# Holding two of ten gather chunks until a Gram product is done, in a DLRM tower kernel

## The reference

```
e = stack([tbl_f[ids[:, f]] for f in range(32)], axis=1)     # 2048 x 32 x 128
dot = einsum('bfd,bgd->bfg', e, e)                           # 2048 x 32 x 32
z = dot[:, iu, ju]                                           # upper triangle, 496 values
h = concatenate([z, dense_ctx], axis=1)                      # 512 values
h = maximum(h @ W_top1 + b_top1, 0)                          # 512
h = maximum(h @ W_top2 + b_top2, 0)                          # 256
y = h @ W_top3                                               # 1
```

## Time and profile before

| | us |
|---|---|
| median of 3 runs | 624.3 (624.0 to 625.61) |
| the profiled execution | 620.44 |
| its span, first to last instruction | 618.5 |
| PE busy | 458.5 (74%) |
| POOL busy | 324.9 (53%) |
| DVE busy | 259.9 (42%) |
| ACT busy | 126.9 (21%) |
| mean granted TensorE clock | 0.865 of full speed |

### The profile page before, as it was taken

How to read it: one execution, slowest core, us unless ns; L and a number is a source line. 1 busy time by engine, 2 the same in 40 slices (tenths; PEclk the granted TensorE clock), 3 DMA queues, 4 the chain that set the end, 5 groups by cost and what they waited for, 6 DMA issues and landing times.

```text
span 618.5 us, 11060 instructions
## 1 busy us (share of the span) xinstructions
PE 458.5 (74%) x4564; PEld 413.5 (67%) x4564; DVE 259.9 (42%) x489; ACT 126.9 (21%) x220; POOL 324.9 (53%) x324
## 2 busy tenths in 40 slices
PE   0785310697787795987967886877969878679998
PEld 0785300587676794867856785857858777669977
DVE  3685000277232641536523472425425364328340
ACT  2361100022211221112301221112212113113323
POOL 6887777156643664446646566436655466450000
PEclk9798655698978897978979978779989789799999
DMA  7996312023312252113422223122521234121000
GB/s 162 244 231 178 101 51 54 10 63 82 76 38 48 56 93 55 34 43 76 72 51 59 51 71 77 34 42 55 98 51 34 47 72 79 48 59 19 2 2 1
DMA packets 31292, 42.08 MB, mean 68 GB/s; under 512 B 11076, under 2 KB 24140, under 8 KB 31272
## 3 DMA queue, kind: packets, MB, share of 16 engines
q1 hardware_dynamic: 18936, 20.64, 16.2%
q0 software_dynamic: 10240, 20.99, 13.9%
q10 hardware_dynamic: 2096, 0.17, 0.3%
HBM read 41.77 MB, written 0.01 MB: 68 GB/s over the span
## 4 chain that ended last, share of the span: by engine, by line
PE 53%; issue 19%; another core or an unknown queue 12%; POOL 7%; DVE 5%; ACT 2%; DMA 2%; DVEq 0%; POOLq 0%
PE sel_ps L280 19%; PE gram_ps L299 17%; PE work_ps L333 7%; POOL gathered L240 7%; PE work_ps L262 4%; DVE onehot L602 3%; DVE pairs L613 2%; PE work_ps L324 1%; DMA gathered<-table,tile_ids 1%; ACT rows_T L458 1%; PE work_ps L407 1%; PE work_ps L316 1%; PE work_ps L341 1%; PE work_ps L416 1%
## 5 line engine op out<-in xcount | busy, mean ns | idle before, releaser
L240 POOL DMA_INDIRECT gathered<-table,tile_ids x320 | 324.7, 1015 | 229.3 <-issue 94.2
L280 PE MATMUL sel_ps<-onehot,table_hi 125*128 125x256 f32 x768 | 205.8, 304 | 47.0 <-DVE onehot L602 26.4
L602 DVE TENSOR_SCALAR onehot<-id_rows,row_no 128x512 fp32r<-128x512 int32 x384 | 160.5, 484 | 129.2 <-remote 85.1
L280 PE MATMUL sel_ps<-onehot,table_lo 125*128 125x256 f32 x768 | 201.0, 298 | 0.0
L280 PEld LDWEIGHTS sel_ps<-onehot,table_hi 125*128 125x128 f32 x768 | 159.3, 207 | 49.4 <-issue 27.7
L299 PE MATMUL gram_ps<-rows_T 128*64 128x64 f32 x1920 | 104.0, 259 | 95.0 <-issue 88.2
L299 PEld LDWEIGHTS gram_ps<-rows_T 128*64 128x64 f32 x1920 | 88.6, 168 | 112.0 <-issue 111.7
L280 PEld LDWEIGHTS sel_ps<-onehot,table_lo 125*128 125x128 f32 x768 | 159.3, 207 | 0.0
L613 DVE STREAM_TRANSPOSE pairs<-gram_ps 32x1024 f32<-32x1024 f32 x60 | 74.7, 1246 | 194.4 <-PE gram_ps L299 193.5
L458 ACT ACTIVATE rows_T<-work_ps 128x512 f32<-128x512 f32 x80 | 47.4, 593 | 187.6 <-PE work_ps L262 139.6
L467 ACT ACTIVATE rows_T<-sel_ps 128x512 f32<-128x512 f32 x48 | 30.6, 637 | 173.1 <-PE sel_ps L280 79.4
(11 more groups left out here) (26 smaller groups left out, 90.2 us busy)
## 6 DMA issues: line engine op xcount, KB each, us to landing
id_rows<-ids_selected SPq DMA_DIRECT2D x48, 256.0 KB
gathered<-table,tile_ids POOLq DMA_INDIRECT x320
pairs<-tables_selected SPq DMA_DIRECT2D x6, 448.0 KB
x<-tables_selected SPq DMA_DIRECT2D x6, 448.0 KB
w_sb<-w SPq DMA_DIRECT2D x1, 1024.0 KB
w_sb<-w SPq DMA_DIRECT2D x1, 512.0 KB
pairs<-tables_selected SPq DMA_DIRECT2D x6, 52.0 KB
x<-tables_selected SPq DMA_DIRECT2D x6, 52.0 KB
```

The source lines that it names most:

```text
L240: nc.gpsimd.indirect_dma_start(gathered[:, t, g, :], None, tables_gathered[g], bass.IndirectOffsetOnAxis(ap=slot_id, axis=0)).then_inc(chu ...
L280: last_op = nc.tensor.matmul(sel_ps[:, u % 2, e, :], part[0:SEL_P, 2 * u + e, k, :], onehot[0:SEL_P, h, kk, e, :], start=(e == 0 and k == ...
L602: last_op = nc.vector.tensor_scalar(onehot[:, h, kk, :, :].rearrange("p e s -> p (e s)"), id_rows[:, slot, :, :].rearrange("p e s -> p (e ...
```

## The change

GpSimd's stream gets two more waits for every pair after pair 0. Before the first gather of chunk 5 it also waits until the first gram of the pair before is done, and before the first gather of chunk 9 until its second gram is done. Nothing else is different; no instruction changes its place.

```
                         if p > 0:
 
                             pool.wait_ge(chunk_turned, 2 * NC * (p - 1) + NC * t + c + 1)
+                            if NC * t + c in (5, 9):
+
+                                pool.wait_ge(gram_done, 2 * (p - 1) + (1 if c == 0 else 2))
                         pool.nop(nofuse=True)
```

## The result

The changed kernel is slower: 638.8 us median (635.2 to 642.2, four runs) against 624.9 us for the kernel before, ratio 1.0244 (95% interval 1.0199 to 1.029). I had forecast 609 us, faster, with a range up to 643 us; the time is near that of my rival A (641 us).

What follows compares the result with a forecast made beforehand. The prediction took PE's stream, with holes in grams beside gathers, as the bound: 620.44 - 12.6 (six pairs) - 2.5 (pair 0) = 605.3 us, plus 3.9 to the median gives 609.2 us; range 577 to 643.

Steps and rivals of the forecast that it cites:

- rival A: Longer gather runs, over the second gram and after it, cost more than free first grams bring: 641 us; chance 0.27.
- First grams: First grams of pairs 1 to 6, freed of eight gathers: -8.0 us a pair, saving between 5.2 and 9.0.
- Second grams: Sixteen held gathers run into second grams of pairs 1 to 6: loss 3.9 us a pair, between 2.3 and 5.3.
- Second gram to next first gram: Stretch behind second grams, run of 12 gathers, not 8: loss 2.0 us a pair, from gain 3.8 to loss 5.2.
- Sum of a pair: Each loop pair: -8.0 + 3.9 + 2.0 = -2.1 us; six pairs give -12.6 us.
- Pair 0: First gram ends 20.0 us earlier, but moved gathers over its second gram give that back: -2.5 us (-4.5 to +1.3).
- B: PE is held only inside grams and late wake-ups shrink with the waits: -10.4 us a pair, 557 us; chance 0.15.
- C: Gathers do not stop a gram, only their time of day coincides, so nothing moves: 624 us; chance 0.05.
- The rule: DMA never contends with a compute engine, so gathers do not stop grams and holding them returns nothing: time as before.

Runs made afterwards that it cites:

- Hold5_7: Changed kernel with chunk 7, not 9, waiting for the second gram: 627.4 us, ratio 1.0062 to the kernel before on chip 10; 0.9988 on chip 1.
- hold5: Changed kernel with only the wait before chunk 5 kept: ratio 0.9987 to the kernel before, where that takes 467 us.
- hold9: Changed kernel with only the wait before chunk 9 kept: ratio 0.9987 to the kernel before, where that takes 467 us.
- paced: Kernel before with a small GpSimd write and wait behind each gather from pair 1 on: 578.9 us, 0.9568 on chip 14; 527.2 us, 1.1299 on chip 3.

## Why the prediction was wrong

The sum said -15.1 us, and +14.9 was measured: 30.0 us apart. Of these, the second grams make 17.9, the six stretches after them 18.6, and the last stretch and the tail 0.9; the first grams give back 5.9 and pair 0 1.5. So two terms failed, by about as much each.

*First grams: right.* -8.0 forecast, (23.9 - 77.8) / 6 = -9.0 measured. Each fell to the row without gathers, though the load of id rows stayed; that load cost these grams nothing.

*Second grams: the first step that failed.* I had both ends: 25.1 us after the first gram if PE starts and is stopped inside, 28.2 if ACT's copy is late, and wrote "I take 3.9, between them". All six pairs went by the late copy: start 24.27 after the first gram (my 24.2), and then 5.47 us for the gram and not 4.0, because PE had idled 10 us and began at the lower clock. The end came at 29.7 us, +6.9, beyond the +5.3 that I had as the worst. The trace of before had ACT's copy of chunk 9 late in every pair of the loop (2.9 to 4.1 us after the turn), as rows 9 show for one; I weighed it as one of two possibilities when nothing spoke for the other. Hold5_7 shows the cause: eight gathers there, and the start is back at 13.1 us.

*Second gram to next first gram: the second step that failed.* +2.0 forecast, (205.1 - 179.1) / 5 = +5.2 measured, the bad end of my range. The mechanism that I had given for that end came true where I had taken it for the worst case: in four of these five stretches GpSimd stops after 8 gathers, since the turn of chunk 1 is seen late (the copy of it 5.0 to 5.8 us after the turn), and once more after the next four. Only after pair 2's second gram do the 12 gathers run through, with 3.03 us of waiting behind them, and that stretch is no shorter (41.8 us). Either way chunk 2's first gather comes 19.0 to 19.4 us after the second gram, where it came 14.9 to 15.8 us after it.

*Sum of a pair:* -2.1 forecast; -9.0 + 10.3 - 3.4 + 5.2 = +3.1 measured. *Pair 0:* -2.5 forecast, -4.0 measured; its first gram ended at 98.0 (forecast 99.3) and its second at 125.3 (124.8 to 130.6).

*The rivals.* A was right: the two losses of a pair passed the gain of the first gram. That its 641 us lie so near the 638.8 measured is in part luck: its terms were -7.0, +5.3 and +4.4, and -9.0, +6.9 and +5.1 (over all six stretches) were measured, so that a gain and two losses, all too small, nearly made up for each other. B fell: the stretches after the second gram became longer, not shorter. C fell where the change was first timed, since the grams did come free. On the five chips at 467 us its outcome came, but for another reason: gathers hold up no gram there, and GpSimd meets both waits when they are already over. I did not think of that as a matter of the chip, and no row of one profile could have told it.

*The rule.* "PE and ACT never wait on anyone" (the Trainium skill, "SBUF — State Buffer", section "Who interferes with whom") holds on chip 1, where a gram takes 4.00 us beside gathers, and not on the first, 13 and 14, where a first gram takes 12 to 14 (on 14 beside spaced gathers). The section speaks of ports of SBUF. No profile here says whether it is a port that PE waits for.

*What stays open.* Why four of nine placements hold PE's signals beside gathers and five do not. Nothing in the kernel, the DMA packets' times or the length of a gather beside a gram (0.94 to 0.95 us on both) tells them apart. What holds PE back is open as well: the reading above, something that fills and is emptied slowly, is untested. The variants hold5 and hold9 were never met on a chip of the slower kind, so the two waits are told apart there only by the table above, and paced has not been combined with a hold. Chip 14's 608 us lie below the 622 to 625 of the others of its kind, and there is no profile of the kernel before there. No chip was used at two times, so what I call the chip's could also be the moment's.

## What to carry to other kernels

A hold moves work; it does not remove it. Before you hold a queue back out of one place, count what has piled up behind the hold and lay that run over what comes next: here 16 gathers of 1.25 us over a gap of 14. When a wake-up is late after every run in the profile of before, price it as certain and as growing with the run. And time a change on more than one chip before you explain it: here one kernel has two bounds, PE held up by gathers or GpSimd's stream, 25% apart, and a change can help on one kind and cost on the other (spaced gathers: some 4% faster and 13% slower).

## What the runs showed of the hardware

- The same kernel took 466 to 467 us on five chips (1, 3, 7, 8, 11) and 608 to 625 us on the other four placements (10, 13, 14 and the first comparison, whose chip is not on record), with the runs of one place within some 2%.
- On the slower kind, in a run of gathers at 1.25 us, a turn 3.7 us into a run of 16 was heard after 0.3 us, one 5 us into a run of 8 after 5.0 to 5.8 us, and one 8 us into a run of 16 after 14.8 us, behind the run's end. GpSimd's own wait behind a run was 2.3, 3.0 and 4.4 us for 8, 12 and 20 gathers.
- On that kind a first gram of the loop ran 50 to 58 of its products in its first 2 us beside gathers and only then slowed; pair 0's slowed down to 11 in 20 us.
- On that kind, 17% more distance between gathers (1.46 us) removed the late wake-ups at chunks 2 to 6 (0.33 us at most, not 4.1), but not the one behind a first gram (2.1 to 4.5 us), and did not shorten the first grams of the loop; pair 0's fell from 52.3 to 22.4 us.
- A gram that starts after 10 us of idleness took 5.2 to 6.3 us at granted clocks of 0.59 to 0.74, against 3.95 us at 1.00.
